# Layer one in three split products, and Q transformed ahead of the transposes

## The reference

```
x = x + autocorrelation(norm(x), ctx, ctx)    # 8 heads of 64: FFT correlation, top 8 shifts, softmax, weighted shifts of V
x = x + (norm(x) @ W.T + bias + LoRA sum)     # "layer one": 512 -> 512
x = x + grouped_attention(norm(x), ctx, ctx)  # 32 query heads, 8 key heads
x = x + moe_ffn(norm(x))                      # 512 -> 1024 -> 512, a routed path, a final layer norm
```

## Time and profile before

| | us |
|---|---|
| median of 3 runs (775.92 to 775.98) | 775.92 |
| the profiled execution | 776.95 |
| its span, first to last instruction | 775.1 |
| TensorE busy in it | 708.1 (91%) |
| ScalarE busy | 492.4 (64%) |
| VectorE busy | 473.3 (61%) |
| GpSimd busy | 362.7 (47%) |

### The profile page before, as it was taken

The page is one execution under the profiler, slowest core; times in us unless marked ns, Lnnn a source line. Parts: engine busy times, 40 slices in busy tenths (PEclk is TensorE's granted clock), DMA queues, the critical chain, the costliest instruction groups (busy, mean ns, idle before and its releaser), DMA issues.

```text
span 775.1 us, 12226 instructions
## 1 busy us (share of the span) xinstructions
PE 708.1 (91%) x3824; PEld 487.6 (63%) x3824; DVE 473.3 (61%) x1136; ACT 492.4 (64%) x865; POOL 362.7 (47%) x446
## 2 busy tenths in 40 slices
PE   3888999999988468899999999999999999999894
PEld 2334445544444346677877777777778778777673
DVE  1567768787771555656666666665765765765412
ACT  2466666575641786786786786786786786786210
POOL 1165785465553331444454454444544534635323
PEclk9999999999999678999999999999999999999997
DMA  8354322232221311101101001011011011000000
GB/s 279 104 110 137 136 82 82 87 105 70 81 68 69 112 55 41 41 2 55 34 22 55 28 26 54 10 44 41 14 54 41 14 54 41 27 14 27 1 14 28
DMA packets 26086, 45.69 MB, mean 59 GB/s; under 512 B 3233, under 2 KB 5025, under 8 KB 26049
## 3 DMA queue, kind: packets, MB, share of 16 engines
q1 hardware_dynamic: 26048, 45.24, 18.6%
HBM read 36.84 MB, written 8.39 MB: 58 GB/s over the span
## 4 chain that ended last, share of the span: by engine, by line
PE 79%; ACT 5%; POOL 4%; issue 4%; DVE 4%; DMA 2%; SPq 1%; POOLq 0%; DVEq 0%; ACTq 0%
PE ps_b L977 7%; PE ps_b L979 7%; PE ps_b L978 7%; PE wide L1083 6%; PE wide L977 4%; PE wide L978 4%; PE wide L979 4%; PE ps_b L1161 3%; PE bank L1055 3%; PE wide L1045 3%; PE ps_a L1023 3%; PE ps_b L1023 3%; PE bank L977 2%; PE ps_a L977 2%; PE ps_a L978 2%
## 5 line engine op out<-in xcount | busy, mean ns | idle before, releaser
L597 POOL TENSOR_TENSOR va<-mv,small 128x1 f32<-128x1 f32 x80 | 15.3, 191 | 205.5 <-DVE mv L957 98.4
L408 ACT ACTIVATE q_stack<-qt_h 32x512 fp32r<-32x512 f32 x128 | 80.6, 630 | 1.9
L1083 PE MATMUL wide<-w_m,x1t 128*128 128x512 f32 x128 | 60.8, 619 | 0.7 <-ACT x1t L429 0.7
L977 PE MATMUL ps_b<-down_h,ht_h 128*128 128x512 f32 x128 | 53.7, 419 | 4.8 <-DVE ht_l L881 3.4
L889 DVE RECIPROCAL y<-ps_b 128x256 f32<-128x256 f32 x32 | 56.0, 1751 | 0.0
L686 POOL TENSOR_TENSOR y_l<-y,y_h 128x512 fp32r<-128x512 f32 x16 | 20.6, 1289 | 72.9 <-ACT y_h L541 72.9
L977 PE MATMUL wide<-up_h,t_h 128*128 128x512 f32 x128 | 53.0, 414 | 1.1 <-DVE t_l L868 1.1
L672 POOL TENSOR_TENSOR kbd_b<-kt_h,small 128x512 bf16<-128x512 f32 x32 | 34.2, 1093 | 37.8 <-ACT kt_h L510 37.8
L912 DVE TENSOR_TENSOR x<-ps_b,x_res 128x512 f32<-128x512 f32 x16 | 11.1, 692 | 66.8 <-PE ps_b L979 66.8
L978 PE MATMUL wide<-up_l,t_h 128*128 128x512 f32 x128 | 51.2, 400 | 0.0
L979 PE MATMUL wide<-up_h,t_l 128*128 128x512 f32 x128 | 51.2, 400 | 0.0
(11 more groups left out here) (184 smaller groups left out, 2088.7 us busy)
## 6 DMA issues: line engine op xcount, KB each, us to landing
ctx_t<-in_ctx SPq DMA_DIRECT2D x32, 256.0 KB, 2.8
x_in<-in_x SPq DMA_DIRECT2D x16, 256.0 KB, 2.7
x_res<-in_x SPq DMA_DIRECT2D x16, 256.0 KB, 2.7
x_in<-x_rows SPq DMA_DIRECT2D x16, 256.0 KB, 2.6
x_res<-x_rows SPq DMA_DIRECT2D x16, 256.0 KB, 3.5
out<-stage SPq DMA_DIRECT2D x16, 256.0 KB, 2.0
stage<-in_L_ffn_up_w SPq DMA_DIRECT2D x2, 1024.0 KB, 5.2
x_rows<-x SPq DMA_DIRECT2D x8, 256.0 KB, 2.6
```

Source lines behind the costliest of these rows:

```text
L408: last = act.activation(out[STACK * part:STACK * (part + 1), p, :], halves[STACK * p:STACK * (p + 1), :].bitcast(F32), ACT.Copy)
L977: pe.matmul(out_ps, w_hi, m_hi, start=start, stop=False)
L1083: last = pe.matmul(bank[7], cols(x1t, c, P), cols(w0_m, c, D), start=(c == 0), stop=(c == DC - 1))
```

## The change

x1t and the merged W are each split into a high and a low half in fp32r, and ffn becomes twelve fp32r matmuls (three for each of four chunks) in place of four f32 matmuls. ScalarE reads the transposed x twice from PSUM: once rounded into x1t_h, once plain into x1t; GpSimd subtracts the two into x1t_l. TensorE's ffn waits for x1t_l. On ScalarE both copies come behind qf; on GpSimd the difference comes behind wgt and ahead of the norms. The merged W is added in place (w0_sum), then ScalarE copies its four chunks to w0_h and GpSimd subtracts them to w0_l, all in step -2. And the Q transform of a tile moves from the head of step i (tile i+2) to the step before, between ffn and xT (written as tile i+3). New semaphores: w0_hi, w0_lo, xt_hi, xt_lo, the last two in place of xt_s.

```
 ScalarE, body(i)
-                t = i - 1
-                if live(t):
-                    act.wait_ge(S["xt_ps"], t + 1)
-                    wait(act, S["ffn_ps"], t)
-                    act.activation(x1t[:], bank[5], ACT.Copy).then_inc(S["xt_s"], 1)
                 t = i + 2
...
                     act.activation(qf[:], ps_a[:], ACT.Copy).then_inc(S["qf_s"], 1)
+                t = i - 1
+                if live(t):
+                    act.wait_ge(S["xt_ps"], t + 1)
+                    wait(act, S["ffn_ps"], t)
+                    act.activation(x1t_h[:], bank[5], ACT.Copy)
+                    wait(act, S["xt_lo"], t)
+                    act.activation(x1t[:], bank[5], ACT.Copy).then_inc(S["xt_hi"], 1)
 ScalarE, peeled(-2), ahead of the copies ex_fc2
+                    for c in range(DC):
+                        act.wait_ge(S["w0_add"], c + 1)
+                        act.activation(w0_h[:, c * D:(c + 1) * D], w0_sum[:, c, :], ACT.Copy).then_inc(S["w0_hi"], 1)
 GpSimd, body(i), between wgt and the norms
+                t = i - 1
+                if live(t):
+                    pool.wait_ge(S["xt_hi"], t + 1)
+                    wait(pool, S["ffn_ps"], t)
+                    pool.tensor_tensor(x1t_l[:], x1t[:], x1t_h[:].bitcast(F32), ALU.subtract).then_inc(S["xt_lo"], 1)
 GpSimd, step -2
+                    for c in range(DC):
+                        pool.wait_ge(S["w0_hi"], c + 1)
+                        k = slice(c * D, (c + 1) * D)
+                        pool.tensor_tensor(w0_l[:, k], w0_sum[:, c, :], w0_h[:, k].bitcast(F32), ALU.subtract
+                                           ).then_inc(S["w0_lo"], 1)
 TensorE, body(i)
                 t = i + 2
                 if live(t):
-                    pe.wait_ge(S["xn1_s"], t + 1)
-                    wait(pe, S["prod2_s"], t - 1)
-                    transform(ps_a, Q0, xn1).then_inc(S["q_ps"], 1)
                     pe.wait_ge(S["ctx_loaded"], 16 * (t + 1))
...
                 t = i - 1
                 if live(t):
-                    pe.wait_ge(S["xt_s"], t + 1)
+                    pe.wait_ge(S["xt_lo"], t + 1)
                     wait(pe, S["x2_raw"], t)
                     if t == 0:
-                        pe.wait_ge(S["w0_add"], DC)
+                        pe.wait_ge(S["w0_lo"], DC)
                         pe.wait_ge(S["rt_lo"], DC)
                     for c in range(DC):
-                        last = pe.matmul(bank[7], cols(x1t, c, P), cols(w0_m, c, D), start=(c == 0), stop=(c == DC - 1))
+                        last = split_product(bank[7], cols(x1t_h, c, P), cols(x1t_l, c, P),
+                                             cols(w0_h, c, D), cols(w0_l, c, D), c == 0, c == DC - 1)
                     last.then_inc(S["ffn_ps"], 1)
...
+                t = i + 3
+                if live(t):
+                    pe.wait_ge(S["xn1_s"], t + 1)
+                    wait(pe, S["prod2_s"], t - 1)
+                    transform(ps_a, Q0, xn1).then_inc(S["q_ps"], 1)
                 t = i
                 if live(t):
                     pe.wait_ge(S["xn2_s"], t + 1)
```

More of the change, by code:

```diff
@@ L168, in build @@
         dft = one("dft", [P, DFT])
-        w0_m = one("w0_m", [P, DC * D])
+        w0_h, w0_l = one("w0_h", [P, DC * D], F32R), one("w0_l", [P, DC * D], F32R)
         b0_all = one("b0_all", [P, D])
@@ L187, in build @@
         xn2 = one("xn2", [P, D])
+        x1t_h, x1t_l = one("x1t_h", [P, D], F32R), one("x1t_l", [P, D], F32R)
         x1t = one("x1t", [P, D])
@@ L231, in build @@
             const_in dft_loaded first_in merge_in lora_in bcast_in stage_in gate_split
-            coef_ready bt_ready ef_ps ef_ready w0_ps w0_add rt_ps rt_hi rt_lo
+            coef_ready bt_ready ef_ps ef_ready w0_ps w0_add w0_hi w0_lo rt_ps rt_hi rt_lo
             stage_hi stage_lo
@@ L236, in build @@
             wt_ps wt_s wf_ps prod2_s o_ps x1_s bn2_s mv2_s va2_s rs2_s xn2_s
-            xt_ps xt_s ffn_ps x2_raw x2_res x2_s x2_stored x2_odd_stored""".split()
+            xt_ps xt_hi xt_lo ffn_ps x2_raw x2_res x2_s x2_stored x2_odd_stored""".split()
         S = {name: sem(name) for name in SEMS}
@@ L241, in build @@
         block = ctx.enter_context(nc.Block())
-        def cols(w, c, n):
-            return w[:, c * n:(c + 1) * n]
         def rows(dram, t):
@@ L835, in peeled @@
                         dve.wait_ge(S["w0_ps"], c + 1)
-                        dve.tensor_tensor(cols(w0_m, c, D), bank[6 + c % 2], w0_sum[:, c, :], ALU.add
+                        dve.tensor_tensor(w0_sum[:, c, :], bank[6 + c % 2], w0_sum[:, c, :], ALU.add
                                           ).then_inc(S["w0_add"], 1)
@@ L983, in _, with cols @@
             pe.wait_ge(S["dft_loaded"], 16)
+            def cols(w, c, n):
+                return w[:, c * n:(c + 1) * n]
             def turn_context(t):
@@ L1059, in body @@
                     pe.wait_ge(S["wgt_s"], t + 1)
-                    wait(pe, S["xt_s"], i)
+                    wait(pe, S["xt_hi"], i)
                     for c in range(DC):
```

## The result

The changed kernel takes 792.53 us (median of 6 runs, 790.38 to 793.84), the kernel before 775.97 beside it: a ratio of 1.021, 95% interval 1.0193 to 1.0228. That is slower, as forecast, but by 16.6 us where 4.6 were forecast, and outside the range of 775.0 to 785.0. The profiled execution took 791.5 with a span of 789.7, 14.6 more than before.

The account below looks back on a forecast made before the run. The prediction took TensorE to bound the steady steps, with other engines and loads deciding the start-up and tail. Its terms summed to +4.6 us, 781.6 profiled and 780.5 as the forecast median, range 775.0 to 785.0.

Parts of the forecast that it names:

- The clock, the term of +1.5: Start-up steps -1 and 0: idle ahead of Q lets TensorE's clock fall once, for part of its length; +1.5, ends 0 to 7.
- First rival, 786: Start-up: clock falls in both gaps and stays low through merge L1115, +7 instead of +1.5, 786.0 us; chance 0.12.
- The order in the start-up, +2.8 +0.85 +2.5 = 6.15: Steps -2, -1 and 0: Q waits for xn1 and holds back the one-off merges; +2.8, +0.85 and +2.5 us.
- rt_l of step 0: Start-up sign: it ends near 68 us; not more than 3 us later than 61.3 would show the prediction wrong.
- The second rival: Start-up: clock holds and TensorE is already fast at tile 1's Q; sum +2.4, 778.3 us; chance 0.22.
- the third (the Wo load covers it): Start-up: the Wo load, not TensorE's merges, sets the time and swallows the delays; sum -3.0, 772.9 us; chance 0.12.
- Steady steps, -5.5: Steps 5 to 12: split products save 0.69 in each ffn, step 12.15 to 11.46; -5.5 us, ends -7.2 and -4.
- The tie with ScalarE's row of copies: Steady steps: ScalarE's copy loop of 11.3 to about 11.45 us ties with TensorE's 11.46; no further gain, nothing lost.
- the fourth rival: Steady steps: ScalarE's loop replaces TensorE's at 12 us or more, the 5.5 shrink to 1; 785.0 us; chance 0.07.
- GpSimd in steps 1 to 4, +1.9: Steps 1 to 4: GpSimd's new difference makes the norms and what follows late; +0.2 in step 1 and +1.7 at corr.
- xn2 of step 3: Step 3 sign: GpSimd's difference stands ahead of the norm, so xn2 waits for nb2 by 1.3 us.
- Step 14 and the tail, +0.6: Step 14's ffn on the chain, -0.7; the last ffn starts 1.9 late but takes 4.9 instead of 5.4, +1.3.

Follow-up runs that it names:

- e4: Changed kernel plus 2, 5 and 7 extra f32 matmuls filling TensorE's idle time ahead of Q in steps -2, -1 and 0; 785.84 us, ratio 1.0116.
- e2: Kernel before with Q alone moved between ffn and xT and x1t's copy behind qf, ffn still four f32 matmuls; 794.63 us, ratio 1.0234.
- e1: Changed kernel with Q back at the head of TensorE's step, split products, copies and differences kept; 776.38 us, ratio 0.9989 against the kernel before.
- e3: Changed kernel with Q in its old place up to tile 3, ahead of the transposes from tile 4 on; 779.72 us, ratio 1.0028.
- e5: e1 with GpSimd's difference x1t_l behind the two norms instead of ahead of them; 797.95 us, ratio 1.0266 against the kernel before.
- e6: e1 with x1t_l made by VectorE straight from PSUM, without ScalarE's second copy and GpSimd's difference; 772.45 us, ratio 0.9940 against the kernel before.

## Why the prediction was wrong

The direction and most of the mechanisms were right. The sum fell short at two of its terms, the clock and the steady steps.

**The clock, the term of +1.5: the step that failed.** It measured 7.5 (the changed kernel against e4, from corr of tile 1 on). I had the two gaps ahead of Q, and took one fall of part of its length. There were three. The fall behind the 1.80 ahead of corr was in no term: I had that lateness in the sum (qf behind the copy ex_fc) but not as a gap. It lengthened corr, wT, V and W0 and made prod2 late, so that the second Q waited for prod2 (2.56) and not, as I had it, for xn1; up to that Q it cost 3.1 (10.20 against e2's 7.12). The second fall cost 1.6 in Q and its merge (6.33 against 4.69), the third 2.7 in Q, xT and the merge (7.82 against e4's 5.08). e2 shows that the first two need not come: there the same gaps passed with the clock up. What decides it stays open. The stated ends of 0 to 7 nearly held the 7.5; the 1.5 was a choice near the low end that no row carried.

First rival, 786: its +7 is near 7.5 in size, though not by what it said. It had both merges at the low level from end to end, 3.6 more each; they took 1.1 and 1.3 more (4.82 and 4.98), and the rest was the work around them. It was the nearest of all and still too low, mostly by the steady steps.

**The order in the start-up, +2.8 +0.85 +2.5 = 6.15.** It measured 6.7. In the changed kernel and in e2 corr of tile 1 comes 3.3 later than before, inside the 2.1 to 4.2 given for step -2, where I had taken 2.8. From it to corr of tile 3 the two steps -1 and 0 add 2.0 and 1.4 in e4, together 3.4. That this matches the 3.35 forecast is luck, since the parts were 0.85 and 2.5. rt_l of step 0 ends at 75.5 where I had set 68. The second rival (+2.4, the clock holds) and the third (the Wo load covers it) have both fallen.

**Steady steps, -5.5.** They gave -2.46. The ffn's saving of 0.69 was sized right, 0.65, and e1 has 5.2 of the 5.5. What was missing is a price for Q's new place in these steps, 0.35 in each: I had counted Q as moved at no cost, from rows in which it stood beside K (1.06 and 0.86 for the pair). The tie with ScalarE's row of copies didn't decide: the steady stretch of the chain is all TensorE. So the fourth rival was right that the 5.5 would shrink, and wrong about the cause.

**GpSimd in steps 1 to 4, +1.9.** 2.01, and xn2 of step 3 waits 1.26 as forecast. In e1, without the start-up's delay, step 3 lost 2.8, as the clock fell behind the same wait; over the four steps e1 lost 2.0 as well.

**Step 14 and the tail, +0.6.** 0.23 from corr of tile 15 to pass two. From the last xT to ffn's copy it is 7.8 us for 6.8, +1.0 where I had +1.3: the ffn starts 1.8 later and takes 4.6, four of its twelve instructions at the fast pitch. The last xT itself comes 0.8 sooner behind corr of tile 15 than before; in e1 it comes 0.7 later, the ffn again 1.8 later behind it, and e1 loses 2.2 in this stretch. Pass two, for which nothing was set, is 0.66 longer, and 0.56 of it is there after its first 11 us. Its first job on TensorE takes 1.11 in the changed kernel and 0.66 before. In e3, where it also takes 0.66, pass two is 0.9 shorter than before; in e1, e2, e4, e5 and e6, where it takes 1.11 or 1.12, it is 0.5 to 1.1 longer. So the clock at the start of pass two goes with it, but that was not tested by itself.

The median rose by 16.6 and the profiled execution by 14.6. Of the 2.0 between them, 1.0 is that the profiled execution of before lay above its median (776.95 against 775.97), and 1.0 that the changed kernel's lay below its own (791.5 against 792.53). The changed kernel's runs lie 3.5 apart. Falls of the clock that come in one execution and not in another would do this, but only one execution of each kernel was traced, and it stays open.

## What to carry to other kernels

Before an operation is moved ahead in an in-order queue, look in the first steps of the pipeline for one-off work behind it: what it gains in the steady state it can lose there many times over. Price each new gap twice, with the clock held and with all the work behind it at the low level: the two ends here lie 7.5 us apart, and equal gaps came out either way. Look for the gaps that the delay itself makes on other engines' waits. Split a change in two (here the split products, -0.65 a step, and Q's place, +0.35 a step and 10 to 14 us at the start) and time each: the good half was hidden under the bad one.

## What was not expected of the hardware

A transform (two row halves, four instructions) takes 1.06 us in the chain with transposes before or behind it, and 0.86 directly behind another transform; four transposes take 0.44 behind the ffn and 0.59 behind a transform. The order alone of the same instructions was 3% of a step. And 28 extra f32 matmul instructions (14 matmuls, some 8 us of TensorE's time) made the kernel 7 us faster (spans 782.9 and 789.7) than without them; with them the granted clock stood at 1.00 from 36 to 80 us.

A fall of the clock didn't follow from the gap ahead of it alone: behind waits of 1.80 and some 2.6 us it fell in the changed kernel and held in e2. Nor does every fall cost. The kernel before has one in its own start-up, in which V of step 0 takes 2.08 for 1.13:

```profile
52.00:54.00 2.00, 2.00 (x8) 0.64 (x4) 0.63 (x2) 1.15 (x2) 0.38 (x3) 0.52 0.22 58
```

e1 has a granted clock of 1.00 in that stretch, and both reach corr of tile 3 at the same time (64.41 and 64.37): e1's TensorE, faster there, then waits 0.80 and 1.03 for ScalarE ahead of Q and K.
